# Four reorderings on two engines: token attention's exponentials, a Gelu and one layer's attention logits against halves of weight splits

## What is computed

```python
x = x + gat(layernorm(x), ...)      # graph layers 0 (8 heads of 768) and 1
x = x + ffn0(layernorm(x), ...)     # routed tokens get 12-head attention, the others a pooled mix; then a 48-wide Gelu net
x = x + gat(layernorm(x), ...)      # graph layers 2 (8 heads of 128, width 1024) and 3
x = x + moe(layernorm(x), ...)      # 8 experts, top 2, and a shared one
x = x + gat12(layernorm(x), ...)    # graph layer 4 (12 heads of 64)
x = x + moe48(layernorm(x), ...)    # 8 experts of width 48, all computed as one product, Gelu, top 2
x = x + gat(layernorm(x), ...)      # graph layers 5 (4 heads of 512, width 2048) and 6
x = x + moe(layernorm(x), ...)      # 8 experts of width 3072, top 2
```

## Time and profile before

| | |
|---|---|
| median of 3 runs | 1204.87 us (1202.83 to 1208.21) |
| the profiled execution | 1205.36 us |
| its span, first to last instruction | 1203.6 us |
| mean granted TensorE clock | 0.994 of full |
| PE busy | 1142.2 us (95%) |
| DVE busy, ACT busy | 581.8 us (48%), 458.5 us (38%) |
| HBM read | 441.73 MB, 367 GB/s over the span |
| chain that ended last | PE 70%, DMA 14%, ACT 5%, SPq 5%, DVE 4% |

### The profile page before, as it was taken

The page is one execution under the profiler, slowest core; times in us unless marked ns, Lnnn a source line. Parts: engine busy times, 40 slices in busy tenths (PEclk is TensorE's granted clock), DMA queues, the critical chain, the costliest instruction groups (busy, mean ns, idle before and its releaser), DMA issues.

```text
span 1203.6 us, 15702 instructions
## 1 busy us (share of the span) xinstructions
PE 1142.2 (95%) x6347; PEld 721.7 (60%) x6347; DVE 581.8 (48%) x892; ACT 458.5 (38%) x525; POOL 22.4 (2%) x48
## 2 busy tenths in 40 slices
PE   8899998989999999989999999999999999889988
PEld 6677784767855455535866686565665655445533
DVE  7877742747644234301665684454554543223410
ACT  4755613515633223201444364343443432222210
POOL 2000010000000000000000000000000000000000
PEclk9999999989999999999999999999999999999999
DMA  9998564864999999999786298999999999999997
GB/s 372 423 407 344 199 246 180 337 266 192 426 425 426 424 425 425 426 420 419 290 311 260 82 428 337 427 425 427 425 424 425 426 426 424 425 426 425 425 423 285
DMA packets 45368, 443.15 MB, mean 368 GB/s; under 512 B 5088, under 2 KB 5248, under 8 KB 11888
## 3 DMA queue, kind: packets, MB, share of 16 engines
q1 hardware_dynamic: 42336, 427.05, 85.5%
q0 software_dynamic: 2960, 15.09, 3.3%
HBM read 441.73 MB, written 0.39 MB: 367 GB/s over the span
## 4 chain that ended last, share of the span: by engine, by line
PE 70%; DMA 14%; ACT 5%; SPq 5%; DVE 4%; issue 1%; POOL 0%; DVEq 0%; ACTq 0%
PE PJ L2036 14%; PE PJ L2005 10%; DMA scratch<-in_weights 9%; PE AC L2073 8%; PE TP L2095 6%; PE PJ L2014 5%; DMA ring<-in_weights 5%; SPq L647 4%; PE AC L1832 3%; PE AC L1820 2%; PE PJ L1996 2%; PE TP L2046 2%; PE MS L1633 1%; PE PJ L1766 1%; PE AC L1811 1%
## 5 line engine op out<-in xcount | busy, mean ns | idle before, releaser
L2036 PE MATMUL PJ<-ring,picked 128*64 128x512 f32 (+1 forms) x588 | 149.7, 594 | 0.0
L915 ACT ACTIVATE low<-PJ 128x512 f32<-128x512 f32 x51 | 30.3, 593 | 242.8 <-PE PJ L2036 170.2
L1391 DVE SCALAR_TENSOR_TENSOR act<-low,CB,PJ 128x512 f32<-128x512 f32 x51 | 38.0, 746 | 159.4 <-PE PJ L2005 84.1
L2036 PE MATMUL PJ<-scratch,picked 128*32 128x512 f32 (+1 forms) x360 | 106.9, 594 | 2.2 <-DMA extra<-in_weights 2.2
L2095 PE MATMUL TP<-ring,extra 128*64 128x512 f32 (+3 forms) x384 | 102.5, 488 | 2.8 <-issue 2.4
L1409 DVE TENSOR_TENSOR ring_lo<-ring,w_lo_u 128x1536 fp32r<-128x1536 f32 x40 | 69.2, 1756 | 52.4 <-ACT w_lo_u L932 52.4
L2095 PE MATMUL TP<-scratch,extra 128*64 128x512 f32 (+3 forms) x320 | 86.5, 489 | 0.4 <-DMA ring<-in_weights 0.4
L932 ACT ACTIVATE w_lo_u<-ring 128x1536 fp32r<-128x1536 f32 x40 | 58.3, 1487 | 66.6 <-DMA ring<-in_weights 30.2
L2036 PEld LDWEIGHTS PJ<-ring,picked 128*64 128x64 f32 (+1 forms) x588 | 42.7, 124 | 55.6 <-issue 54.9
L1409 DVE TENSOR_TENSOR ring_lo<-ring,w_hi_u 128x1536 fp32r<-128x1536 f32 x34 | 58.9, 1755 | 23.4 <-ACT w_hi_u L932 23.2
L2014 PE MATMUL PJ<-ring_lo,XTh 128*128 128x512 f32 x168 | 67.2, 400 | 0.0
(11 more groups left out here) (467 smaller groups left out, 2256.0 us busy)
## 6 DMA issues: line engine op xcount, KB each, us to landing
ring<-in_weights SPq DMA_DIRECT2D x147, 1536.0 KB, 17.6
scratch<-in_weights SPq DMA_DIRECT2D x73, 1536.0 KB, 19.6
extra<-in_weights SPq DMA_DIRECT2D x39, 1536.0 KB, 20.7
extra<-in_attn POOLq DMA_DIRECT2D x11, 768.0 KB, 10.7
ring<-in_weights SPq DMA_DIRECT2D x8, 768.0 KB, 30.1
extra<-in_attn POOLq DMA_DIRECT2D x6, 512.0 KB, 10.7
extra<-in_weights SPq DMA_DIRECT2D x4, 768.0 KB, 25.7
ring<-in_weights SPq DMA_DIRECT2D x8, 384.0 KB, 16.8
```

Source lines behind the costliest of these rows:

```text
L915: A(silu, PJ[:, 0:SEG], ACT.Silu).then_inc(S("silu_ready"), 1)
L1391: v.scalar_tensor_tensor(hexp, silu, weight, PJ[:, SEG:2 * SEG], ALU.mult, ALU.mult) \
L2036: ins = mm(dst[c], x[:, t, c], slab_at(LOAD[q, kind, side])[:, t * SEG:(t + 1) * SEG], start=(t == 0), stop=(t == KT - 1))
```

## The change

In token attention ACT's exponentials come ahead of both halves of slab 32, whose first half now follows them and whose second half follows the copy of the places. In the 48-wide experts the second half of slab 1 moves from before the Gelu to behind the two copies that follow it. On DVE, in layer 2 the first half of slab 3 moves one step up (from t == 2 to t == 1), and in layer 5 the two halves of slab 3 come behind the logits of their steps. No instruction is added or removed; PE's, SP's and POOL's programs are the same.

```diff
             A(V, AC[:, 0:D], ACT.Copy).then_inc(S("v_ready"), 1)
-            narrow_split_hi(0)
             act.wait_ge(S("self_max"), 1)
...
             ins.then_inc(S("self_exps"), 1)
+            narrow_split_hi(0, (0,))
             act.wait_ge(S("self_turned"), 1)
             A(ALT[:, 0:3 * P], TP[:, 0:3 * P], ACT.Copy).then_inc(S("self_attn_ready"), 1)
             act.wait_ge(S("places_turned"), 1)
             A(placesT, MS[:, 2 * P:3 * P], ACT.Copy).then_inc(S("places_ready"), 1)
+            narrow_split_hi(0, (1,))
...
             graph_split_hi(0)
-            graph_split_hi(1)
+            graph_split_hi(1, (0,))
             act.wait_ge(S("l2_hidden_product"), 1)
...
             A(CBT[0:E8, :], TP[0:E8, SEG:SEG + P], ACT.Copy).then_inc(S("l2_T_ready"), 1)
+            graph_split_hi(1, (1,))
             keep_x(6)
...
                         narrow_split_lo(2)
-                    if c == 2 and t == 2:
+                    if c == 2 and t == 1:
                         narrow_split_lo(3, (0,))
-                    if c == 5 and t < 3:
-                        graph_split_lo(*((2, (0,)), (3, (0,)), (3, (1,)))[t])
+                    if c == 5 and t == 0:
+                        graph_split_lo(2, (0,))
                     if 0 <= t - 1 < n:
                         logits(c, t - 1)
+                    if c == 5 and 1 <= t < 3:
+                        graph_split_lo(3, (t - 1,))
```

## The result

The changed kernel takes 1195.3 us (median of 4 runs, 1194.53 to 1196.79), the kernel before 1204.7 beside it (4 runs, 1202.83 to 1208.21): ratio 0.992, 95% interval 0.9895 to 0.9945. The predicted 1195.3 and faster by over 0.5% came out. The profiled execution after is one of 1195.46 us with a span of 1193.7, 9.9 less than the span before.

The account below looks back on a forecast made before the run. The chain of waits, mostly PE and weight stream, was taken as the bound, with ACT and DVE on it in short stages. 4.7 + 1.2 + 0.8 + 2.6 + 0.6 + 0.2 = 10.1 off 1205.36 gives 1195.3 us; range 1192.0 to 1201.0.

Parts of the forecast that it names:

- What bounds the kernel: Whole kernel: the chain of waits that ended last, mostly PE and weight stream; ACT and DVE only in short stages.
- part 4: Layer 5 on DVE: logits come ahead of slab 3's halves; gain 0.2 us, between 0 and 0.9.
- Part 1: Token attention on ACT: exponentials ahead of slab 32's halves; 4.7 us of wait and 1.2 of PE's slow clock saved.
- Part 2: Layer 2 on DVE: half moved into idle time; 0.8 us of order and 2.6 of PE's half clock saved.
- Part 3: 48-wide experts: Gelu with one ACT half fewer ahead; gain 0.6 us, stopped by DVE's low halves of slab 0.
- Is it kept?: Mixtures: time saved ahead is kept, as SP waits 21.7 us for the order of experts before the full-rate stream.
- The clock rival: Layer 2: the clock falls again, or the median before did not hold the fall; 1197.9 us, chance 0.24.
- Given back: Stages shorten but slab 33's or the mixture's transfer ends as before, or the stream decides; 1201.2 to 1204.9, chance 0.16.
- No order gain: Token attention: table load is held with the maxima, 3.6 us of wait still saved; about 1196.4, chance 0.02.
- Slower: Layer 2: moved half waits for ACT's half of slab 35 and delays the logits; 13 us late gives 1207, chance 0.03.

Follow-up runs that it names:

- b_only: Kernel before with only the 48-wide experts' edit, one ACT half moved behind the Gelu; 1204.51 us, ratio 0.9995.
- work_only: Changed kernel with two ACT copies of the halves' size put back ahead of the exponentials, without the wait for slab 32; 1201.01 us, ratio 0.9945.
- warm_l2: Kernel before, order untouched, with 7 filler matmuls on PE ahead of layer 2's first segment transposes; 1204.09 us, ratio 0.9993.
- c_only: Kernel before with only the layer 2 edit on DVE; 1204.12 us, ratio 0.9983.
- no_c: Changed kernel with the layer 2 edit on DVE taken out; 1198.59 us, 3.15 above the changed kernel beside it.
- wait_only: Changed kernel with only the wait for slab 32's landing put back ahead of ACT's exponentials; 1198.02 us, ratio 0.9937.
- d_only: Kernel before with only the layer 5 edit on DVE; 1204.90 us, ratio 0.9992.
- a_only: Kernel before with only the token attention edit on ACT; 1199.66 us, ratio 0.9949.
- more_gelu: Changed kernel with the second low half of slab 0 (DVE) moved behind the weighting of the Gelu; 1196.07 us.
- best: Changed kernel with slab 32's halves behind the places copy, slab 0's second low half behind the Gelu's weighting, fillers ahead of layer 2's transposes; 1195.49 us, ratio 0.9908.

## Why the prediction came out right

**What bounds the kernel** held: the gains lie in the stages that were named, and the chain there is shorter by them (part 4's in a part of the profiles only).

**Part 1** (4.7 of wait and 1.2 of clock, 5.9) measured 6.34 against the profiled execution before. The mechanism is the one given: the load at 191.84, exponentials from 193.13, PE without a gap, the halves behind them free, the next slab's half without a wait. But the 4.7 was read from one execution as if it were the kernel's. Of it 2.6 is ACT's work and always there (b_only, work_only), the rest is the landing, 0 to 2.0. The 1.2 is the same kind of number: 2 of the 5 executions without part 1 paid nothing for the clock there, and warm_l2 some 2.4 on the 8 matmuls. The mean of the five, 5.1 for wait and clock together, lies 0.8 below the 5.9 predicted.

**Part 2** (0.8 of order, 2.6 of clock) measured 0.83 (1.61 to 0.78) and 2.62 (warm_l2), 3.43 together in c_only. That it would be 0.8 and not the half's 1.67 was right, because the activation also waits for PE's segment. That part 1 alone would already bring 1.1 of this, because the clock falls later behind it, the prediction did not have; it changes which part the gain belongs to and not the sum. For the 2.3 then left to part 2 no_c's total gives 3.15, from six runs on either side, which can't tell the two apart.

**Part 3** (0.6) measured 0.71, stopped by DVE's low halves as said. **Part 4** (0.2) differs by 0.33 in the two profiles compared, all of it in the second segment, but this is 0.2 of order and the rest an earlier landing. The prediction saw the vectors' wait of 1.00 and took it for fixed; it moves between 0.23 and 1.91, and from 1.00 on it decides the step, so part 4's 0.2 is often not there.

**Is it kept?** Through the first mixture, yes: from layer 2's second product to the mixture's last product (L2153, L2157 after) it is 561.24 - 258.05 = 303.19 before and 303.39 after. Through the second, not quite: from the up-projections' first long row to the end of the span 522.8 before, 524.1 after, 1.2 of the 11.1 lost in the stream. That looks like scatter and not like an effect of the change: the changed kernel's second profile takes 522.5 there, less than the kernel before, and all profiles lie between 521.9 and 524.5 without regard to the edit.

So the terms against the profiled execution were 6.3 + 3.4 + 0.7 + 0.3 = 10.8 where 10.1 was predicted, 0.4 came from an earlier start, 0.2 were lost in the first mixture and 1.2 in the second's stream: 9.9, to a tenth. That 1195.3 was hit exactly is partly luck. With part 1's mean in place of the one execution the terms are 5.1 + 3.4 + 0.7 and 0 to 0.2, some 0.7 to 0.9 less than the 10.1 predicted; and the medians of the kernel before were 1204.7, 1205.87, 1205.52 and 1207.69 in four sets of runs, so that its distance from the changed kernel was 9.4 the first time and 12.25 when both ran again. What the runs do bear out is each step's mechanism, and a gain of about 10.

**The rivals.** The clock rival fell: layer 2's clock did not fall in any profile with a gap of 0.78. Its other half, that the fall before might not always be there, fell too, 5 of 5. Given back: 1.2 in the profiled execution, nothing in the changed kernel's second profile, and never the 5.9. No order gain (the table load held by the maxima) did not happen in the changed kernel, but wait_only shows its price, 1.14, as forecast. Slower: ACT and DVE were done with slab 35's half ahead of the logits (0.35 of DVE's idle time is left); how late that slab may land was not tried.

By the rule that the prediction drew on (the Trainium skill, TensorE: Matmul & The Clock Gate, Part 1: idle time throttles PE, and the place varies from run to run) the trace agrees in both halves, but each at its own place: in layer 2 the fall came with the gap every time, in attention it came behind a gap of 2.57 (work_only) and did not behind one of 3.51 (d_only). Within layer 2 the place varied too: at the transposes in three profiles (1.10 to 1.12 for them), behind them in a_only and no_c (0.66).

## What to carry to other kernels

A gap that ends with a transfer's landing has two parts: the work behind the landing, which is there every time, and the landing, which is only as long as in the execution that was profiled; size them apart, from more than one profile. Moving the work that waits for a transfer behind the work that does not takes away both, and here some of the spread from run to run went with them. The same holds for a gain beside such a wait: part 4 shows only where the transfer is early. Where TensorE stands in a short gap and runs at half clock behind it, price the gap and the clock separately, and try fillers in the gap: they show the clock's share without touching the order.

## What the runs showed of the hardware

The spread was not expected. Kernels in which ACT must wait for slab 32 ahead of the exponentials spread over 6.9 to 11.5 us (before 1198.45 to 1209.97 in 31 runs, b_only, c_only and d_only over 8.7 to 10.4 in 12, warm_l2 over 6.9 in 12, wait_only over 6.9 in 7); the others over 2.3 to 4.8 (a_only 3.7 in 8, work_only 3.6 in 8, no_c 2.8 in 6, more_gelu 4.6 and best 4.4 in 6, the changed kernel 2.3 in 4 and 4.8 in 6). A range grows with the number of runs, so the standard deviations say it better: 2.6 over the 110 runs of the five kernels without part 1, 2.5 in wait_only, 1.6 over the 36 runs of the six that have part 1 and nothing put back (each run against its own set's mean), 1.2 in work_only. The landing moves by 2 us in the profiles, so it may be a part of this; the clock behind the gap, 2.75 to 5.18 for the same 8 matmuls, is another. No run separates them. In wait_only's one profile the slab was not waited for, so that its wide spread comes from the landing is not shown.

Most of the scatter goes with the clock: over the 62 runs of the kernel before, in three sets, the time is 7.4 us longer for each 0.01 of mean granted clock less (correlation -0.90).

The mean granted clock was 0.990 over the 31 runs of the kernel before (0.986 to 0.999) and 0.996 over the first four of the changed one (0.993 to 0.999). Further stretches below 1.00 came and went in the profiles without regard to the edit: 40 to 50 (0.83 in c_only and wait_only), 520 to 540, 580 to 630, and, in all 14, one or more between 1070 and 1160, where the weight stream is in the chain of waits. What these last ones cost was not measured. What lets the clock fall at these was not looked for.

A second wait ahead of an activation made its table load wait as well (193.98 instead of following L988 at once), 1.14 us; this is one run.
